# Accumulating forms for VectorE's SBUF-only instructions, fewer idle products, and an earlier copy of a head pair's sums

## The reference

```
x = x + self_attention(layernorm(x))            # one head of 128, out projection
x = x + cross_attention(layernorm(x), ctx)      # 16 heads of 64, 1601 context rows of 96 channels
x = x + ffn(layernorm(x))                       # see below

cross_attention: q = x Wq; k = ctx Wk; v = ctx Wv
                 softmax(q k^T / 8) v, heads joined, then Wo + bo
ffn:   weights = x router_w + router_b          # one score a token
       the 31 tokens with the highest scores of each sequence are chosen;
       only they go through rmsnorm, rope, 16-head attention with a mask,
       rmsnorm, gelu MLP of 512, times their score; every other token stays as it is
```

## Time and profile before

| what | value |
|---|---|
| median of 3 runs | 2214.22 us |
| lowest and highest | 2211.22 and 2214.97 us |
| the profiled execution: its time, its span | 2211.51 us, 2210.3 us |
| PE busy | 2130.7 us (96%), 22150 products |
| DVE busy | 1789.7 us (81%), 3744 instructions |
| ACT busy | 1830.5 us (83%), 3125 |
| POOL busy | 1924.6 us (87%), 1111 |
| mean granted PE clock | 0.997 of full speed |

### The profile page before, as it was taken

One profiled execution on the slowest core, in us unless ns is written; L12 is line 12 of the kernel. 1 busy time (PEld: TensorE's weight loads), 2 busy tenths in 40 slices (PEclk: granted clock), 3 DMA queues, 4 the chain that ended last, 5 costly groups with the idle time before them and its releaser, 6 DMA issues.

```text
span 2210.3 us, 58078 instructions
## 1 busy us (share of the span) xinstructions
PE 2130.7 (96%) x22150; PEld 1555.6 (70%) x22150; DVE 1789.7 (81%) x3744; ACT 1830.5 (83%) x3125; POOL 1924.6 (87%) x1111
## 2 busy tenths in 40 slices
PE   8999999999999999999999999999999999999988
PEld 5677777777777767777777776777777777777665
DVE  7788879788887888878787898877878788886755
ACT  6898888889888888888888887888888888888862
POOL 3899999999998989899899898988989898998982
PEclk9999999999999999999999999999999999999999
DMA  3110000000000000000000000000000000000000
GB/s 74 41 37 13 2 13 2 2 13 2 13 2 13 2 2 13 2 13 2 11 13 2 13 2 2 13 2 13 2 21 3 2 13 2 2 2 2 2 9 13
DMA packets 17363, 22.21 MB, mean 10 GB/s; under 512 B 5616, under 2 KB 14976, under 8 KB 17088
## 3 DMA queue, kind: packets, MB, share of 16 engines
q1 hardware_dynamic: 15984, 18.30, 3.0%
q10 hardware_dynamic: 1104, 0.20, 0.1%
HBM read 16.27 MB, written 2.10 MB: 8 GB/s over the span
## 4 chain that ended last, share of the span: by engine, by line
PE 67%; DVE 12%; ACT 10%; issue 7%; POOL 2%; DMA 0%; SPq 0%; DVEq 0%; ACTq 0%; POOLq 0%
PE PS L567 12%; PE PS L607 12%; PE PS L568 11%; PE PS L584 10%; PE PS L586 9%; PE PS L630 4%; DVE EH L1071 4%; DVE over L1094 3%; ACT PF L889 3%; ACT over L911 2%; ACT EH L896 2%; POOL EL L1550 2%; PE PS L617 2%; PE PS L640 2%; DVE junk L1345 1%
## 5 line engine op out<-in xcount | busy, mean ns | idle before, releaser
L1550 POOL TENSOR_TENSOR EL<-PF,EH 124x1024 f16<-124x1024 f32 x828 | 1759.4, 2148 | 196.4 <-DVE EH L1071 108.0
L889 ACT ACTIVATE PF<-PS 124x512 f32<-124x512 f32 x1664 | 973.3, 603 | 223.9 <-PE PS L568 212.3
L584 PE MATMUL PS<-Ch,EH 123*128 123x97 f16 (+1 forms) x6656 | 765.2, 207 | 23.1 <-POOL EL L1550 12.3
L586 PE MATMUL PS<-Cl,EL 123*128 123x97 f16 (+1 forms) x6656 | 761.9, 207 | 0.0
L1071 DVE TENSOR_SCALAR_CACHE_REDUCE EH<-PF 124x1024 f16<-124x1024 f32 x621 | 745.3, 1209 | 7.7 <-ACT PF L889 7.6
L584 PEld LDWEIGHTS PS<-Ch,EH 123*128 123x128 f16 (+1 forms) x6656 | 607.8, 98 | 188.6 <-issue 61.6
L586 PEld LDWEIGHTS PS<-Cl,EL 123*128 123x128 f16 (+1 forms) x6656 | 597.3, 98 | 168.2 <-issue 0.8
L1094 DVE CUSTOM_DVE_ANT_1 over<-over,PS 128x806 f32<-128x806 f32 x512 | 506.1, 988 | 190.4 <-ACT over L911 113.1
L567 PE MATMUL PS<-AH,ChT 97*124 97x512 f16 x1664 | 644.8, 387 | 8.5 <-ACT PF L889 5.6
L568 PE MATMUL PS<-AL,ClT 96*124 96x512 f16 x1664 | 633.0, 380 | 0.0
L911 ACT ACTIVATE over<-PS 128x806 f32<-128x806 f32 x512 | 434.1, 848 | 32.8 <-PE PS L607 11.8
(11 more groups left out here) (234 smaller groups left out, 1812.9 us busy)
## 6 DMA issues: line engine op xcount, KB each, us to landing
Cf<-in_ctx SPq DMA_DIRECT2D x16, 546.0 KB
X<-in_x SPq DMA_DIRECT2D x16, 128.0 KB, 2.5
out_x<-X SPq DMA_DIRECT2D x16, 128.0 KB, 1.7
msk<-in_attention_mask SPq DMA_DIRECT2D x4, 256.0 KB, 4.5
AH<-mh SPq DMA_DIRECT2D x63, 2.0 KB
Cf<-in_ctx SPq DMA_DIRECT2D x16, 53.6 KB
xWqT<-in_xWqT SPq DMA_DIRECT2D x2, 256.0 KB, 6.6
xWo<-in_xWo SPq DMA_DIRECT2D x2, 256.0 KB, 4.0
```

Of the source, the lines that this page charges most:

```text
L584: pe.matmul(PS[:, 6, u0:u0 + DC + 1], EH[0:kr, r, qs], Ch[j][0:kr, t, :], start=(t == 0 and q == 0), stop=False, skip_group_check=True)
L586: m = pe.matmul(PS[:, 6, u0:u0 + DC + 1], EL[0:kr, r, qs], Cl[j][0:kr, t, :], start=False, stop=(t == KT - 1), skip_group_check=True)
L889: act.activation(PF[:, n % PRING, :], PS[0:KP, 4 + n % 2, :], ACT.Exp).then_inc(sg("ex"), 1)
L1550: pool.tensor_tensor(EL[:, r - 1:r + 1, :], PF[:, f - 1:f + 1, :], EH[:, r - 1:r + 1, :], ALU.subtract).then_inc(sg("lo_pool"), 1)
```

## The change

There are three edits.

1. Each SBUF-only DVE instruction named above takes a form that also adds up (or takes the maximum of) its results into one column of a new tile `unread`, which nobody reads; `spill` hands out its 32 columns in turn. `tensor_scalar` with one operation takes `accum_out`; `tensor_tensor` becomes `tensor_tensor_reduce`; `scalar_tensor_tensor` takes `accum_out`; and `normalize`, which has two operations, becomes a `scalar_tensor_tensor` whose second tensor is the inverse deviation, broadcast. The two instructions of `scale_queries` become one, for which `gback` is kept a second time, multiplied by `KEEP`, in `gtop`.
2. `STREAM_BUSY` asks for 3, 3 and 2 idle products in place of 7, 11 and 3: 8 a group in place of 21.
3. In `whole_order`, `av` of a tile is put ahead of `round` and `lo` of the same tile.

The diff, cut to its core:

```
-        if n % 2 and ROUND_LAG <= n < TOTAL + ROUND_LAG:
-            put(n, "round", n // 2 - ROUND_LAG // 2)
-        if n % 2 and LO_LAG <= n < TOTAL + LO_LAG:
-            put(n, "lo", n // 2 - LO_LAG // 2)
         late = n - AV_LAG
         if late >= 1 and late % KT == 1:
             put(n, "av", late - 1)
         if late >= 0 and late % KT:
             put(n, "av", late)
+        if n % 2 and ROUND_LAG <= n < TOTAL + ROUND_LAG:
+            put(n, "round", n // 2 - ROUND_LAG // 2)
+        if n % 2 and LO_LAG <= n < TOTAL + LO_LAG:
+            put(n, "lo", n // 2 - LO_LAG // 2)
...
-            STREAM_BUSY |= {("base", 4 * gq + 6, 7): 7, ("c_thid", gq): 11, ("c_scat", gq, 0): 3}
+            STREAM_BUSY |= {("base", 4 * gq + 6, 7): 3, ("c_thid", gq): 3, ("c_scat", gq, 0): 2}
...
+            def spill():
+                nonlocal spilled
+                spilled += 1
+                return unread[:, spilled % UNREAD:spilled % UNREAD + 1]
...
-                    m = dve.tensor_scalar(dst_of(t), X[:, T * b + t, :], mv[:, which, t, 0:1],
-                                          rstd[:, which, t:t + 1], ALU.subtract, ALU.mult)
+                    m = dve.scalar_tensor_tensor(out=dst_of(t), in0=X[:, T * b + t, :], scalar=mv[:, which, t, 0:1],
+                                                 in1=rstd[:, which, t:t + 1].to_broadcast([P, D]), op0=ALU.subtract,
+                                                 op1=ALU.mult, accum_out=spill())
...
-                dve.tensor_scalar(qscale[:, 0, j, halves], gback[:, halves], u_scale[:, j:j + 1], None, ALU.mult)
-                dve.tensor_scalar(qscale[:, 1, j, halves], gback[:, halves], u_scale[:, j:j + 1], KEEP, ALU.mult,
-                                  ALU.mult).then_inc(sg("q_scale"), 1)
+                dve.tensor_scalar(qscale[:, :, j, halves], gback[:, :, halves], u_scale[:, j:j + 1], None, ALU.mult, ALU.add,
+                                  accum_out=spill()).then_inc(sg("q_scale"), 1)
...
-                    dve.tensor_tensor(X[:, T * b:T * b + T, :], X[:, T * b:T * b + T, :],
-                                      xbo[:, :].rearrange("p (o d) -> p o d", o=1).to_broadcast([P, T, D]),
-                                      ALU.add).then_inc(sg("bo_added"), 1)
+                    dve.tensor_tensor_reduce(out=X[:, T * b:T * b + T, :], in0=X[:, T * b:T * b + T, :],
+                                             in1=xbo[:, :].rearrange("p (o d) -> p o d", o=1).to_broadcast([P, T, D]),
+                                             scale=1.0, scalar=0.0, op0=ALU.add, op1=ALU.add,
+                                             accum_out=spill()).then_inc(sg("bo_added"), 1)
...
-                        m = dve.tensor_scalar(GT[:, b % 4, t, :], slots[:, :], rank[:, j, t:t + 1], None, ALU.is_equal)
+                        m = dve.tensor_scalar(GT[:, b % 4, t, :], slots[:, :], rank[:, j, t:t + 1], None, ALU.is_equal,
+                                              ALU.add, accum_out=spill())
...
-                                             op1=ALU.mult).then_inc(sg(f"c_hn{n}"), 1)
+                                             op1=ALU.mult, accum_out=spill()).then_inc(sg(f"c_hn{n}"), 1)
...
-                    dve.tensor_scalar(XA[:, :], XA[:, :], XS[:, D:D + 1], None, ALU.mult).then_inc(sg("c_proc"), 1)
+                    dve.tensor_scalar(XA[:, :], XA[:, :], XS[:, D:D + 1], None, ALU.mult, ALU.add,
+                                      accum_out=spill()).then_inc(sg("c_proc"), 1)
```

More of the change, by code:

```diff
@@ L63 @@
 LEAST = -3.0e38
+UNREAD = 32
 PI = 3.1415925
@@ L421, in build @@
         esum = sb("esum", [KP, ERING // 2])
+        unread = sb("unread", [P, UNREAD])
         x_dram = a["x"].rearrange("b (p t) d -> p b t d", t=T)
@@ L1274, in vector_program @@
                                       ALU.add).then_inc(*own_step())
-                    dve.tensor_scalar(gback[:, q:q + 1], e, 2.0 ** -SHIFT * DH ** -0.5, None, ALU.mult)
+                    for n, keep_of in enumerate((1.0, KEEP)):
+                        dve.tensor_scalar(gback[:, n, q:q + 1], e, 2.0 ** -SHIFT * DH ** -0.5 * keep_of, None, ALU.mult)
                     w.wait_ge(*own_steps())
@@ L1399, in vector_program @@
                               .to_broadcast([P, 2 * FH, FD // 2]) for x in range(2))
-                    dve.tensor_tensor(dst[:, :, 0, :], src[:, :, 0, :], co, ALU.mult)
-                    dve.tensor_tensor(dst[:, :, 1, :], src[:, :, 1, :], co, ALU.mult)
-                    dve.tensor_tensor(rt[:, 0, :, :], src[:, :, 1, :], si, ALU.mult)
-                    dve.tensor_tensor(rt[:, 1, :, :], src[:, :, 0, :], si, ALU.mult).then_inc(*own_step())
-                    w.wait_ge(*own_steps())
-                    dve.tensor_tensor(dst[:, :, 0, :], dst[:, :, 0, :], rt[:, 0, :, :], ALU.subtract)
-                    dve.tensor_tensor(dst[:, :, 1, :], dst[:, :, 1, :], rt[:, 1, :, :], ALU.add).then_inc(sg("c_rope"), 1)
+                    for half in range(2):
+                        dve.tensor_tensor_reduce(out=dst[:, :, half, :], in0=src[:, :, half, :], in1=co, scale=1.0, scalar=0.0,
+                                                 op0=ALU.mult, op1=ALU.add, accum_out=spill())
+                    for half in range(2):
+                        m = dve.tensor_tensor_reduce(out=rt[:, half, :, :], in0=src[:, :, 1 - half, :], in1=si, scale=1.0,
+                                                     scalar=0.0, op0=ALU.mult, op1=ALU.add, accum_out=spill())
+                    m.then_inc(*own_step())
+                    w.wait_ge(*own_steps())
+                    dve.tensor_tensor_reduce(out=dst[:, :, 0, :], in0=dst[:, :, 0, :], in1=rt[:, 0, :, :], scale=1.0,
+                                             scalar=LEAST, op0=ALU.subtract, op1=ALU.max, accum_out=spill())
+                    dve.tensor_tensor_reduce(out=dst[:, :, 1, :], in0=dst[:, :, 1, :], in1=rt[:, 1, :, :], scale=1.0,
+                                             scalar=0.0, op0=ALU.add, op1=ALU.add,
+                                             accum_out=spill()).then_inc(sg("c_rope"), 1)
                 elif k == "c_val":
@@ L1415, in vector_program @@
                     for b4 in range(4):
-                        dve.tensor_tensor(
-                            KX[:, b4, :, :],
-                            fqkT[:, 1, rows[b4]].rearrange("p (o k) -> p o k", o=1).to_broadcast([P, FH, CAP]),
-                            headmask[:, :].rearrange("p (h o) -> p h o", o=1).to_broadcast([P, FH, CAP]),
-                            ALU.mult).then_inc(sg("c_kx"), 1)
+                        dve.tensor_tensor_reduce(
+                            out=KX[:, b4, :, :],
+                            in0=fqkT[:, 1, rows[b4]].rearrange("p (o k) -> p o k", o=1).to_broadcast([P, FH, CAP]),
+                            in1=headmask[:, :].rearrange("p (h o) -> p h o", o=1).to_broadcast([P, FH, CAP]),
+                            scale=1.0, scalar=0.0, op0=ALU.mult, op1=ALU.add,
+                            accum_out=spill()).then_inc(sg("c_kx"), 1)
                 elif k == "c_sc":
```

23 lines of the change are left out of this document (13 added, 10 removed).

## The result

The changed kernel took 2199.7 us (median of 4 runs, 2198.1 to 2204.1), the kernel before 2214.3 in the same comparison (4 runs, 2211.2 to 2215.0): a ratio of 0.994, 95% interval 0.9927 to 0.9952. That is 14.6 us faster. The forecast was 2168, a gain of 46; the time lies at the upper edge of the range of 2150 to 2200, and its place is that of the first rival (2190) rather than of the forecast.

A forecast was written before the change was run, and what follows sets the result against it. PE's own list of products was taken as the bound (2130.7 us busy of 2210.3). Terms summed to 45.2 us, taking 2211.5 to 2166.3; 2.7 more for the median gave 2169, stated as 2168, range 2150 to 2200.

The forecast's parts named there:

- the first rival: DVE forms with two SBUF inputs still wait for POOL despite the accumulator; gain 24 us, time 2190; chance 0.21.
- The step that failed: DVE's SBUF-only instructions: an accumulator frees two-input forms from waiting for POOL, as it does one-input L1071; chance 0.62.
- Edit 3, 10.6 us: Copy `U` ahead of the rounding, once a batch: PE no longer loses 0.66 us in each of 16 waits.
- `c_thid`, 5.6: PE's transposes behind L1383: freed, it releases PE 1.85 us earlier in each of three groups, 5.6 us.
- `base`, 2.5: The fold behind L1433: freed, it releases PE 0.84 us earlier in each of three groups, 2.5 us.
- Third `c_scat`, 7.9: L1459 freed at the third group: PE's 3.35 us stand goes, full clock gives back up to 4.5; sum 7.9 us.
- Scatters, 0.4: One idle product fewer at each `c_scat`, counted for two groups: 0.4 us gained.
- the cost of the forms, -0.8: Accumulating forms add 0.5 us in DVE's serial tail and 0.3 for two more instructions in each `gtop` at the start.
- Stream waits, 19: PE's 61 waits for POOL, the count and the fold: half of 39 us comes back, 19; bounds 0 and 39.
- Edit 2: 39 fewer idle products, 8.4 us, not added to the `c_thid` and `base` terms; nothing there if the stalls stay.
- slower: the clock: PE's stands at `c_thid`, `base` or in the stream drop the clock, 4.5 us each; nine falls: 2230; chance 0.06.
- given back: All forms freed, but PE then waits for ACT or a full POOL queue; time 2190; chance 0.06.

## Why the prediction was wrong

**The step that failed** is the sentence of edit 1 "I take them as freed too, because what L1071 shares with them is the accumulator." It carried 0.62 of the chances. L1060, L1250, L1397, L1436 and L1454 show it false (they still reach 2215, 1552, 2203, 2505 and 1516 ns; before 2179, 1554, 2207, 2504 and 1511). What counts is the number of SBUF inputs: one with an accumulator is free (`GT`, `qscale`, `XA`, and in the experiments the normalization, `hn` and the keys), two are not, one in PSUM and one in SBUF is free. The first rival said so by the rule of the Trainium skill, page "SBUF — State Buffer", section "SBUF: two separate sides", that VectorE takes the shared port pair in a 2-port mode or with two SBUF inputs; every line measured here agrees with its second half. That one-input forms get free by an accumulator is in line with the first half (a plain `GT` waits, 1002 ns, an accumulating one doesn't), but these runs don't tell a change of mode from other effects of the accumulator. L1328, the one row that looked like evidence for free two-input forms, had never lain beside a subtraction; that was said, and then outvoted by an argument from likeness. Where it does meet one, in the kernel with all forms freed, it waits (372 to 396 ns in place of 280 to 294).

Term by term, by the runs:

- **Edit 3, 10.6 us: measured 6.1.** The site returned 0.64 us; the batch kept 0.41, in the batch laid out above the rest was lost in two steps within 20 us behind the site. The error was counting a local stop at its full length in all 16 places.
- **`c_thid`, 5.6: nothing**, since L1397 waits as before. Freed with the gains in the copies, a batch with it got 0.74 us shorter, some 2.2 in the three, so this term would have been about 2.5 times too large even in its own world: of the 1.85 us a site, 0.82 show up again as a wait for POOL.
- **`base`, 2.5: nothing**; L1454 has 1.52 us, before 1.51.
- **Third `c_scat`, 7.9: measured 8.4** by one accumulator alone (7.2 by the last stretch of the profiles, 101.9 to 94.7 us). Both halves of the term, the 3.35 us stand and the clock behind it, came out.
- **Scatters, 0.4, and the cost of the forms, -0.8**: below what the runs resolve. The reading of an accumulator, put at up to 0.1 us in a chain, costs 0.02: two `GT` that wait for nothing start 0.17 us apart with it and 0.15 without. Two comparisons bound the cost: with and without the two-input forms 2199.7 and 2199.2, with and without all of the stream's 2196.3 and 2196.1.
- **Stream waits, 19: about nothing.** The wait of the `EL` product for POOL didn't fall (16.4 us, before 12.3; 13.0 in the run with only the one-input forms, which takes the same time). In the world with all forms freed, c_scat and edit 3 taken off, 37.3 - 8.4 - 6.1 = 22.8 us remain for `c_thid`, `base` and the stream, where the terms had 27.1. Between the changed kernel and that one, 13.3 came from the chosen tokens' chain and 10.4 from all else: the stream term was sized at nearly twice what it holds with these forms free.
- **A term that was missing: the keys.** L1436 (L1416 before) builds the keys in four steps of up to 2505 ns, and PE's scores wait for them; no term counted it. Freed by the reading from PSUM it shortened the batch with the keys by 1.9 us, three times in the stream (4.2 us by the medians), and by 2.7 together with the first forms of the rotation; `c_thid` and `base` together had been given 8.1. That the total of the freed world came out near the forecast is luck in part: this missing term stood against the oversized ones.
- **Edit 2** was put at nothing if the stalls stay. It cost 1.0 to 1.2 us, at the edge of what the runs tell: PE's stand of 2.1 us at `c_thid` was followed by 3.41 us at 1.2 GHz in 8 of 15 cases. The rival "slower: the clock" had this mechanism with 4.5 us for each fall; each was worth about 1.6 (136.23 against 134.64 for the batch), so six would have made 10 us and not 27, and it couldn't decide the sign. Three sites at 8 in 15 and 1.6 us each would make 2.6 us a launch, more than the 1.0 to 1.2 between the medians; a trace is one execution, and how often the timed runs fell isn't known.

6.1 + 8.4 - 1.0 = 13.5 of the measured 14.6 us. The rest, 1.1, is within the runs' spread and not assigned.

**The first rival** was right in mechanism and put the gain at 24: edit 3 at 10.6 was 4.5 too much, and its share of the stream, 6, was 6 too much. A DVE stall that is taken off one instruction in the stream turns up at a plain or two-input one further on (L1379 behind `GT`; `keep` once the normalization is free; `KD`, 639 ns before, 849 after and 1455 once nearly all are free). That this goes on as long as POOL's subtractions follow each other without a gap is argued from these three and not tested.

**The "given back" rival** was right in kind and in the wrong place: waits for POOL, 88% busy, take back more than half of what `c_thid` gains once it is freed.

## What to carry to other kernels

When an instruction looks freed by one feature, check the feature on a row that has the same number and place of inputs; a row that never met the disturbance is no evidence. A wait at a shared resource that is almost always held isn't removed from a stream by freeing one user: look for the next user, and count gains only at places where another engine is waiting for that very instruction. The cheapest parts here, one accumulator on the instruction that PE stood for and one line moved, made the whole gain. Ahead of a step that stays late, idle products are not time to be won; they keep the clock.

## What was not expected of the hardware

- The reading of an accumulator takes 0.07 to 0.09 us and costs the chain 0.02: it runs beside the end of its instruction, and behind an accumulating `GT` (244 ns) the next instruction starts after 0.17 us, behind a plain one that didn't wait after 0.15.
- Stands of PE and the clock: 2.1 us at `c_thid` was followed by one stretch of 3.41 us at 0.50 in 8 of 15 cases, 1.1 us at `base` in none; the same kernel had it at some sites and not at others. 3.35 us at the third `c_scat` before was followed by 10.24 us. With edit 3 alone the stand there was 3.3 us and the half clock lasted 13.65.
- Within the first 24 us some executions show half clock and others none: the fourth copy of sums starts at 118.2 us (after) and 119.8 (before) without it, and at 120.4 to 122.4 in the six profiles where 6.8 or 10.2 us ran at 0.50 there. What chooses was not found, and 2 to 3 us between two single profiles mean nothing for that reason.
- Still open: a plain one-input form that is kept from POOL's port in another way than by an accumulator, which would tell the accumulator from the mode.
